# Three token-row scatters in flight instead of two, in a four-layer gated cross-attention kernel

## The reference, cut to what matters

```python
def _L1_ffn_ref(x, w_router, w1, w3, w2, ws1, ws3, ws2):
    xf = x.reshape(-1, D_MODEL)                      # 2048 tokens x 256
    scores = jax.nn.softmax(xf @ w_router, axis=-1)  # 8 experts
    expert_weights, expert_indices = jax.lax.top_k(scores, TOP_K)   # TOP_K = 2
    ...
    h = jax.nn.silu(jnp.einsum('td,edh->teh', xf, w1)) * jnp.einsum('td,edh->teh', xf, w3)
    y = jnp.einsum('teh,ehd->ted', h, w2)
    moe_out = jnp.einsum('te,ted->td', cw, y)
    shared = jax.nn.silu(xf @ ws1) * (xf @ ws3) @ ws2
    out = shared / (TOP_K + 1) + moe_out * (TOP_K / (TOP_K + 1))
x = x + jnp.tanh(g_ffn[1]) * _L1_ffn_ref(_layernorm(x, axis=-1), ...)
```

## Time and profile before

| | us |
|---|---|
| median of 3 runs | 718.2 (716.95 to 722.09) |
| the profiled execution, its own time | 717.92 |
| its span in the profile | 716.1 |
| PE busy in the span | 691.5 (97%) |
| DVE busy | 384.0 (54%) |
| ACT busy | 287.8 (40%) |
| POOL busy | 132.9 (19%) |

### The profile page before, as it was taken

How to read it: one execution, slowest core, us unless ns; L and a number is a source line. 1 busy time by engine, 2 the same in 40 slices (tenths; PEclk the granted TensorE clock), 3 DMA queues, 4 the chain that set the end, 5 groups by cost and what they waited for, 6 DMA issues and landing times.

```text
span 716.1 us, 11166 instructions
## 1 busy us (share of the span) xinstructions
PE 691.5 (97%) x3616; PEld 477.2 (67%) x3617; DVE 384.0 (54%) x947; ACT 287.8 (40%) x598; POOL 132.9 (19%) x111
## 2 busy tenths in 40 slices
PE   8899999999899999999999999999999999999996
PEld 8667777777653444698999646656455766666665
DVE  4678877788623445788778556221233333333321
ACT  3555434443544645776777441111222222222220
POOL 3100000000000000600000004660123334333333
PEclk9999999999999999999999999999999999999999
DMA  9780000000052000005701101323563666665642
GB/s 297 183 262 15 1 0 0 0 0 0 1 168 68 0 6 4 1 1 211 260 0 31 58 1 68 131 92 94 158 185 69 166 163 161 162 162 162 163 99 32
DMA packets 54933, 65.15 MB, mean 91 GB/s; under 512 B 11582, under 2 KB 37904, under 8 KB 54894
## 3 DMA queue, kind: packets, MB, share of 16 engines
q1 hardware_dynamic: 47806, 55.31, 23.9%
q0 software_dynamic: 7088, 9.35, 7.4%
HBM read 48.48 MB, written 16.00 MB: 90 GB/s over the span
## 4 chain that ended last, share of the span: by engine, by line
PE 82%; DMA 7%; DVE 5%; issue 3%; ACT 2%; POOL 1%; POOLq 0%; SPq 0%; DVEq 0%; ACTq 0%
PE ps L567 71%; PE ps L570 11%; DMA expert_rows<-middle,row_index 5%; DMA work<-expert_rows 1%; POOL expert_rows L528 1%; DVE stats L1678 1%; DMA early<-in_wk 1%; DVE x_rows L1940 0%; ACT work L1276 0%; DVE work L1967 0%; ACT work L1346 0%; POOLq L133 0%; DVE x_rows L1976 0%; DVE work L1831 0%; DVE den L1829 0%
## 5 line engine op out<-in xcount | busy, mean ns | idle before, releaser
L567 PE MATMUL ps<-middle,work 128*128 128x256 f32 (+4 forms) x656 | 177.5, 420 | 3.5 <-DVE work L2277 1.3
L1276 ACT ACTIVATE work<-ps 128x512 f32<-128x512 f32 (+3 forms) x209 | 83.1, 437 | 207.5 <-PE ps L570 194.4
L567 PEld LDWEIGHTS ps<-middle,work 128*128 128x128 f32 (+1 forms) x656 | 115.7, 183 | 51.1 <-issue 32.1
L567 PE MATMUL ps<-late,work 32*128 32x154 f32 (+5 forms) x880 | 142.0, 345 | 0.6 <-ACT work L1276 0.6
L533 POOL DMA_INDIRECT out_rows<-masks x47 | 70.4, 1498 | 159.5 <-DMA out_rows<-masks 58.0
L567 PEld LDWEIGHTS ps<-late,work 128*128 128x128 f32 (+2 forms) x880 | 92.4, 179 | 6.4 <-issue 3.4
L570 PE MATMUL ps<-consts_sb,work 128*128 128x128 f32 (+1 forms) x564 | 80.2, 279 | 6.9 <-DVE work L1967 2.6
L567 PE MATMUL ps<-work,late 128*128 128x256 f32 (+1 forms) x416 | 82.9, 352 | 0.5 <-ACT work L1276 0.5
L570 PEld LDWEIGHTS ps<-consts_sb,work 128*128 128x128 f32 (+1 forms) x564 | 65.3, 141 | 26.6 <-issue 14.4
L499 POOL TENSOR_TENSOR rstd<-var_eps,minus_half 128x8 f32<-128x8 f32 (+1 forms) x10 | 13.9, 1392 | 364.5 <-DVE var_eps L1693 364.5
L567 PE MATMUL ps<-early,late 128*128 128x512 f32 (+2 forms) x192 | 77.6, 608 | 0.3 <-ACT early L1415 0.3
(11 more groups left out here) (225 smaller groups left out, 716.5 us busy)
## 6 DMA issues: line engine op xcount, KB each, us to landing
late<-in_w SPq DMA_DIRECT2D x40, 512.0 KB, 4.2
early<-in_w SPq DMA_DIRECT2D x16, 512.0 KB, 10.9
expert_rows<-work SPq DMA_DIRECT2D x36, 130.0 KB, 2.9
work<-expert_rows SPq DMA_DIRECT2D x36, 130.0 KB, 2.1
middle<-in_w SPq DMA_DIRECT2D x8, 512.0 KB, 7.9
out_rows<-x_rows SPq DMA_DIRECT2D x4, 512.0 KB, 3.3
x_rows<-in_x SPq DMA_DIRECT2D x2, 768.0 KB, 10.9
late<-in_ws SPq DMA_DIRECT2D x3, 512.0 KB, 4.0
```

Source lines behind the costliest of these rows:

```text
L567: return nc.tensor.matmul(o, l, r, start=start, stop=stop, **kw)
L1276: return nc.scalar.activation(o, i, ACT.Copy)
```

## The change

A third semaphore `r_scat2` is added and the unused name `f_ev` is taken out. The scatters are counted through, n = 16k + t, and use the three semaphores in turn. Scatter n waits until scatter n-3 has landed. SyncE's two closing waits become three, on 11, 11 and 10 scatters. The scatters themselves, their order and all other instructions are as before.

```diff
-        f_xn f_tx f_ev f_gcx f_gmm f_gact f_cpl ...
+        f_xn f_tx f_gcx f_gmm f_gact f_cpl ...
...
-        r_xn r_tx r_ev ... r_zero r_row r_scat0 r_scat1
+        r_xn r_tx r_ev ... r_zero r_row r_scat0 r_scat1 r_scat2
...
-            sp.wait_ge(q["r_scat0"], T * 16)
-            sp.wait_ge(q["r_scat1"], T * 16)
+            for n in range(3):
+                sp.wait_ge(q[f"r_scat{n}"], (2 * T + 2 - n) // 3 * 16)
...
                 for t in range(T):
-                    after(pool, q[f"r_scat{t % 2}"], 16 * (T // 2 * k + t // 2))
+                    n = T * k + t
+                    after(pool, q[f"r_scat{n % 3}"], 16 * (n // 3))
                     pool.indirect_dma_start(rows_in[:, :], bass.IndirectOffsetOnAxis(ap=idx[k][:, t:t + 1], axis=0),
-                                            trow[:, t, :], None).then_inc(q[f"r_scat{t % 2}"], 16)
+                                            trow[:, t, :], None).then_inc(q[f"r_scat{n % 3}"], 16)
```

More of the change, by code:

```diff
@@ L284, in build @@
         seed_mm seed_row n_seed_mm n_seeds n_pick n_seed n_xn n_tx n_xt n_sc n_sub n_exp n_p n_tp n_pt n_pv n_res
-        f_xn f_tx f_ev f_gcx f_gmm f_gact f_cpl f_l1 f_l2 f_l3 f_l4 f_a1 f_a2 f_a3 f_tanh f_a4 f_prod f_sum f_upd f_bt f_res
+        f_xn f_tx f_gcx f_gmm f_gact f_cpl f_l1 f_l2 f_l3 f_l4 f_a1 f_a2 f_a3 f_tanh f_a4 f_prod f_sum f_upd f_bt f_res
         a_mask a_seed a_xn a_tx a_xt a_qm a_q a_sc a_sub a_exp a_tp a_pt a_pv a_att a_res
-        r_xn r_tx r_ev r_lg r_lgT r_lgx r_lgc r_e r_esc r_mask r_rank r_pos r_zero r_row r_scat0 r_scat1
+        r_xn r_tx r_ev r_lg r_lgT r_lgx r_lgc r_e r_esc r_mask r_rank r_pos r_zero r_row r_scat0 r_scat1 r_scat2
         s_h s_sil s_hs s_y s_res r_exp h_ld0 h_ld1 h_w2 d_ld d_lw d_tx d_xt d_h d_sil d_hh d_y d_yc d_to d_meta e_ld0 e_ld1 e_tx e_xt e_h e_sil e_hh e_th e_hTa e_hTv e_y e_yc e_pick e_meta e_to e_to2 e_add st_out""".split()
```

## The result

The changed kernel took 736.0 us (median of 6 runs, 733.09 to 738.13), the kernel before beside it 718.98 us (median of 6, 716.95 to 722.09). The ratio is 1.0208, with a 95% interval of 1.0167 to 1.0249. So it is slower by 2.1%, some 17 us, and the interval lies clear of 1. The profiled execution took 735.97, with a span of 734.1, which is 18.0 more than the 716.1 of before.

The account below looks back on a forecast made before the run. PE was taken as the bound, busy 97% of the span, with scatters costing it only one stall before the seam's first transpose. Removing 1.68 us (1.52 idle, 0.16 overlap) from the median 718.2 gave 716.5 us, range 714.5 to 719.7.

Parts of the forecast that it names:

- same: Whole kernel: a time within about 1% (7.2 us) of before, the least a measurement can tell; chance 0.96.
- The scatter stage: POOL's scatter loop: 26 waits shrink to gaps of 0.30 us, 6.5 us go, last landing at 478.6 instead of 485.06.
- A fourth in flight would bring nothing: POOL's scatter loop: with three under way POOL's own preparation is the limit, at a pitch of 1.26 us.
- The 1.7 us at the seam: PE after `s_down(2, 1)`: the first transpose of scattered rows starts at 485.71 instead of 487.39, 1.68 us earlier.
- PE, DVE and ACT need no transfer in that stretch: Shared expert beside the scatters: denser scatters, 28% of the DMA engines instead of 24.4%, delay nobody on PE.
- a third transfer finds room: DMA engines during the scatters: share 0.26 without a store, 0.38 at most with one, so mostly idle.
- Rival D: Scatter landings: three in flight slow each other; mild form 719.7 us, outer bound 733.8; chance 0.04.
- Rival B: Scatter landings: the third scatter only queues, landing takes about 4.2 us, the pitch stays, no gain, 718.2 us; chance 0.10.
- Rival C: End of the kernel: the whole 6.5 us won on the scatters comes out there, 711.7 us; chance 0.03.
- 1.7 of 6.5 us: Scatters win 6.5 us; PE gains 1.7, three quarters being hidden under `s_up(3, f)` and `s_down(2, 1)`.
- a pitch of 1.44 us: POOL's scatter loop: the pitch up to which the gain on PE is whole; from 1.496 on there is a loss.

Follow-up runs that it names:

- e1_four: The changed kernel with a fourth semaphore, up to four scatters in flight; 717.62 us, ratio 0.9983 to the kernel before.
- e9_four_again: The changed kernel with up to four scatters in flight, measured once more on another chip; 718.34 us, ratio 0.9936 to the kernel before.
- e17_after_fourth: The changed kernel, unaltered, on a chip without the stall; 718.07 us, ratio 0.9956 to the kernel before.
- e2_pace: The changed kernel with a small POOL memset behind each scatter and no wait, which left the pitch unchanged; 717.02 us, ratio 0.9993.
- e10_paced: The changed kernel with POOL waiting for a memset of its own behind each scatter, pitch 1.42 us; 719.01 us, ratio 0.9946.
- e13_paced_again: The changed kernel with POOL waiting for its own memset behind each scatter, on a chip with the stall, pitch 1.43 us; 717.31 us, ratio 0.9966.

## Why the prediction was wrong

The predicted time was 716.5 us in a range of 714.5 to 719.7, and "same" had 0.96. Measured were 736.0. The sum had no term for signals that come late, and the runs showed one of 15.4 us.

- **The scatter stage** was right. Predicted: gaps of 0.30 us, last start at 476.1 after a first at 436.24, which is 39.8 us (by 29 pitches of 1.26). Measured: 477.8 - 437.8 = 40.0.
- **A fourth in flight would bring nothing**: right. e1_four and e9_four_again have the same pitch as three.
- **The 1.7 us at the seam** was right, even on the chip with the stall (3.46 us from the batch to the transpose instead of 5.13).
- **"PE, DVE and ACT need no transfer in that stretch"** and "a third transfer finds room" is the step that failed. It is true of data. PE, DVE and ACT pass signals to each other all through that stretch, and I took for granted that only the DMA engines' busy share (28% forecast, 28 to 30% measured) is shared between the scatters and the rest. The clue was at hand: I could have asked what a denser row of scatters shares with PE's signals, and priced a delay of them. Nothing in the trace of before gave its size, though: there, the increments of PE that are recorded are on time. But 108 of the 512 landing increments of the scatters are missing from that trace already, and so the view of L528 has no line for the landing times, as that of L533 does. Missing records go with every chip that had the stall.
- **Rival D** had the right sign, and at its outer bound nearly the right time (733.8), but that is luck: its mechanism was wrong. It put the price on slower landings. They didn't slow: POOL found each scatter landed in time. Its chance of 0.04 counted only a mechanism that the trace spoke against. The cost was in a place for which I had no rival at all.
- **Rival B**, and the rule of the Trainium skill on serialized transfers ("DMA: Bandwidth & Descriptors", "Rules for kernel authors"): the trace does not bear it out for whole scatters. POOL never waited for one in the first measurement, and landings in e17_after_fourth and e9_four_again take 2.5 and 2.6 us in the median.
- **Rival C** didn't happen: PE's work was the bound up to the seam on every chip without the stall.
- **On chips without the stall** the times of the changed kernel, 717.32 and 718.07, lie in the stated range, and the seam is as forecast. The gain at the end isn't confirmed in its size. By the ratios of 0.9938 and 0.9956 it is 4.5 us (1.4 to 7.4) and 3.2 us (0.3 to 6.0), which takes in the 1.7. e1_four and e2_pace, with the same pitch, had 0.9983 and 0.9993: 1.2 and 0.5 us, neither clear of nothing, and the interval of e2_pace ends at 1.3.

**The better kernel.** e10_paced, three in flight with a paced POOL, had no stall on either kind of chip: 0.9946 (0.9907 to 0.9985) on chip 0, and, as e13_paced_again, 0.9966 (0.9935 to 0.9997) on chip 6, just clear of 1. It is the only one of the kernels here that was measured faster than the kernel before on both, and the changed kernel is faster only on the kind without the stall.

## What to carry to other kernels

DMA engines that were busy to 30% did not mean here that a denser row of transfers cost nothing: PE's signals to the other engines came late. When a queue of many small indirect transfers is let go faster, look at who exchanges semaphores in the same stretch, and leave a pause if the transfers aren't on the path anyway: here 1.7 of 6.5 us could be won, and by the prediction's own sum a pitch of 1.44 us was enough for it. And when a kernel's time jumps in one measurement and not in the next, run the unaltered kernel again beside each experiment from the first round on, since the chip, or the moment, is one of the variables.

## What was not expected of the hardware

- The same program took 735.58 us on one chip and 717.32 on another, with intervals of 1.0158 to 1.027 and 0.9897 to 0.998 against the kernel before, which itself differed by 0.3% between them (720.59 and 722.75, the other way round).
- An increment of PE came 23 us late (483.26, for matmuls that end at 459.9), and its matmuls went on for 14 of these: DVE's wait was ended by the signal and not by the work, and the profile calls the releaser "remote".
- Instructions that were held back advanced in steps of 0.70 us, PE's matmuls as well as SyncE's increments.
